# Half of the gate and up weight chunks turned by VectorE out of a blocked copy in DRAM, in an AdaLN FFN kernel

## The reference, cut to what matters

```python
def _L0_cond_ref(x, c, weight, c_weight, bias):     # x [128, 32, 512]
    out = lax.conv_general_dilated(x, weight, window_strides=(1,), padding=[(4, 4)],
                                   dimension_numbers=('NCH', 'OIH', 'NCH'), feature_group_count=4)
    ctx = jnp.einsum('nd,od->no', c, c_weight)
    return out + ctx[:, :, None] + bias[None, :, None]

def _L0_ffn_ref(x, W_gate, W_up, W_down):           # W_gate, W_up [1376, 512]; W_down [512, 1376]
    xt = x.reshape(-1, x.shape[-1])
    up = xt @ W_up.T
    gate = jax.nn.silu(xt @ W_gate.T)
    return (gate * up @ W_down.T).reshape(x.shape[:-1] + (W_down.shape[0],))

return x + _L0_ffn_ref(_L0_cond_ref(x, cond_128, ...), W_gate, W_up, W_down)
```

## Time and profile before

| | |
|---|---|
| time, median of 3 runs | 752.04 us (751.13 to 752.36) |
| the profiled execution | 751.72 us, of which its span is 749.9 us |
| PE busy | 739.6 us (99%) |
| DVE, ACT, POOL busy | 379.5, 274.4, 52.4 us |
| granted TensorE clock, mean | 0.999 |
| DMA | 152.37 MB, 203 GB/s over the span |

### The profile page before, as it was taken

How to read it: one execution, slowest core, us unless ns; L and a number is a source line. 1 busy time by engine, 2 the same in 40 slices (tenths; PEclk the granted TensorE clock), 3 DMA queues, 4 the chain that set the end, 5 groups by cost and what they waited for, 6 DMA issues and landing times.

```text
span 749.9 us, 10087 instructions
## 1 busy us (share of the span) xinstructions
PE 739.6 (99%) x3375; PEld 602.4 (80%) x3375; DVE 379.5 (51%) x639; ACT 274.4 (37%) x521; POOL 52.4 (7%) x88
## 2 busy tenths in 40 slices
PE   7999999999999999999999999999999999999998
PEld 6778888878888888887888888887888888887886
DVE  3896766654765454436734545443753333334224
ACT  4565655543433233234322333324431332333221
POOL 4433323210000000000000000000000000000000
PEclk9999999999999999999999999999999999999999
DMA  6496578569977677765544866866443967775413
GB/s 186 114 317 239 187 273 281 186 226 327 354 268 247 216 222 219 197 205 159 167 135 171 282 202 193 244 194 180 162 133 106 312 190 196 194 193 172 141 29 112
DMA packets 115029, 152.37 MB, mean 203 GB/s; under 512 B 12482, under 2 KB 50530, under 8 KB 114978
## 3 DMA queue, kind: packets, MB, share of 16 engines
q1 hardware_dynamic: 114496, 151.51, 64.8%
q10 hardware_dynamic: 482, 0.21, 0.1%
HBM read 108.95 MB, written 34.34 MB: 191 GB/s over the span
## 4 chain that ended last, share of the span: by engine, by line
PE 94%; DVE 2%; DMA 1%; SPq 1%; issue 1%; ACT 1%; POOL 0%; POOLq 0%; DVEq 0%
PE bank L727 55%; PE bank L790 32%; PE bank L645 3%; PE bank L640 3%; SPq L344 1%; PE bank L683 1%; DVE hc_lo L1091 1%; DMA x_in<-in_x 1%; PE bank L606 1%; PE bank L654 1%; PE bank L665 0%; DMA stage<-g_all 0%; DVE g_all L1294 0%; DVE ring L1091 0%; DVE g_all L1192 0%
## 5 line engine op out<-in xcount | busy, mean ns | idle before, releaser
L727 PE MATMUL bank<-hc_hi,ring 128*128 128x512 f32 (+1 forms) x1204 | 374.0, 392 | 1.0 <-issue 1.0
L727 PEld LDWEIGHTS bank<-hc_hi,ring 128*128 128x128 f32 (+1 forms) x1204 | 221.4, 185 | 50.2 <-issue 1.4
L727 PE MATMUL bank<-hc_lo,ring 128*128 128x512 f32 (+1 forms) x602 | 234.8, 390 | 0.0
L790 PE MATMUL bank<-ring,g_hi 128*128 128x512 f32 (+1 forms) x704 | 218.6, 392 | 0.0
L790 PEld LDWEIGHTS bank<-ring,g_hi 128*128 128x128 f32 (+1 forms) x704 | 131.2, 188 | 28.1 <-DVE g_lo L1091 0.8
L859 ACT ACTIVATE mix<-bank 128x512 f32<-128x512 f32 (+1 forms) x129 | 76.7, 594 | 188.0 <-PE bank L727 188.0
L790 PE MATMUL bank<-ring,g_lo 128*128 128x512 f32 (+1 forms) x352 | 137.1, 390 | 0.0
L727 PEld LDWEIGHTS bank<-hc_lo,ring 128*128 128x128 f32 (+1 forms) x602 | 111.5, 185 | 25.8
L1091 DVE TENSOR_TENSOR g_lo<-g_all,g_hi 128x512 fp32r<-128x512 f32 (+1 forms) x88 | 60.4, 689 | 88.6 <-ACT g_hi L859 88.6
L859 ACT ACTIVATE g_hi<-g_all 128x512 fp32r<-128x512 f32 (+1 forms) x88 | 55.1, 629 | 114.1 <-PE bank L790 114.0
L1265 DVE TENSOR_TENSOR mix<-bank,mix 128x512 f32<-128x512 f32 (+1 forms) x43 | 29.7, 691 | 129.4 <-PE bank L727 129.4
(11 more groups left out here) (141 smaller groups left out, 468.7 us busy)
## 6 DMA issues: line engine op xcount, KB each, us to landing
ring<-saved SPq DMA_DIRECT2D x319, 256.0 KB, 3.0
saved<-ring SPq DMA_DIRECT2D x99, 256.0 KB, 3.7
g_all<-in_x SPq DMA_DIRECT2D x32, 256.0 KB, 3.6
out_y<-g_all SPq DMA_DIRECT2D x32, 256.0 KB, 3.7
x_in<-in_x SPq DMA_DIRECT2D x96, 64.0 KB, 2.1
stage<-win SPq DMA_DIRECT2D x96, 64.0 KB, 2.9
w_nat<-in_L_ffn_W_gate SPq DMA_DIRECT2D x10, 256.0 KB, 3.4
w_nat<-in_L_ffn_W_up SPq DMA_DIRECT2D x10, 256.0 KB, 3.4
```

The lines of the kernel that those rows point to most:

```text
L727: mm = pe.matmul(bank[0:w, :], wt, hv, start=fresh and q == 0 and t == 0, stop=q == 1 and t == 2, skip_group_check=not fresh)
L790: mm = pe.matmul(acc(half, tt)[:], gs, wd, start=f == 0 and t == 0, stop=f == FC - 1 and t == 2)
```

## The change

Three things change.

1. Chunks 0 to 4 are turned by PE as before, chunks 5 to 10 (`LATE` = 5) by DVE. For them ACT issues twelve DRAM-to-DRAM DMAs in the steps `k` = 0 to 3 of the prologue (`quarter`), which write W_gate and W_up from row 640 on into a DRAM tensor `quarters`, where the elements of L stand in four blocks, one for each 32 partitions. Eight of them have 1472 rows of 256 bytes (two of these eight 240 bytes), four have 736 rows of 16 bytes. `load_nat` reads `quarters` for these chunks and waits for all six DMAs of its kind, and DVE's `turn_weights` writes `x_gate` and a new tile `up_kept`. PE's turns, ACT's copy from the bank and POOL's `wrap` go for these chunks.
2. In every group the elements of L lie otherwise on the partitions of `stage`: a half of L goes as pairs, even elements in one tile and odd ones in the other. A window's DMA writes 8 partitions with 8 KB each, where it wrote 16 with 4 KB each. PE's turns of chunks 0 to 4 read `w_nat` with a step of two elements.
3. There are two semaphores for `stage` in place of four: one for each half of L. What waited for one tile now waits for both tiles of its half.

The core of the diff:

```diff
+        quarters = nc.dram_tensor("quarters", [2, 4, F, 2 * 2 * QUAD], F32, kind="Internal").ap()
+            up_kept = sb("up_kept", [P, KC, P], F32, early)
+        staged = [half for half in (sem("staged_low"), sem("staged_high")) for _ in range(2)]
-        STAGED = JJ * LD
+        STAGED = 2 * JJ * LD
         def stage_window(queue, grp, i, w):
-            queue.dma_start(stage[w * R:(w + 1) * R, i, :, :].rearrange("r o n -> r (o n)"), windows(grp, i)[:, w, :]
-                            ).then_inc(staged[i], LD)
+            h, row = (i * JJ + w) // (2 * JJ), (i * JJ + w) % (2 * JJ) * R // 2
+            queue.dma_start(stage[row:row + R // 2, 2 * h:2 * h + 2, :, :].rearrange("r i o n -> r (i o n)"), windows(grp, i)[:, w, :]
+                            ).then_inc(staged[2 * h], LD)
...
+                    if f >= LATE:
+                        sp.wait_ge(quartered[kind], 6 * LD)
+                        size = w // QUAD * P
+                        sp.dma_start(w_nat[:, slot, 0:size], quarters[kind, :, f * P:f * P + w, :].rearrange("a (n b) e -> a n (b e)", n=QUAD)
+                                     ).then_inc(nat_loaded[slot], LD)
...
-                    if g == 0 and f + 2 < FC:
+                    if g == 0 and f + 2 < LATE:
                         turn_gate(f + 2)
...
+            def quarter(kind, a):
+                rows, part = (w_gate, w_up)[kind][LATE * P:F, :], quarters[kind, a, LATE * P:F, :]
+                at, size = PAD + 2 * QUAD * a, 2 * QUAD - (PAD if a == 3 else 0)
+                act.dma_start(part.rearrange("f (h e) -> (f h) e", h=2)[:, 0:size],
+                              rows.rearrange("f (h l) -> (f h) l", h=2)[:, at:at + size]).then_inc(quartered[kind], LD)
+                if a == 3:
+                    for h in range(2):
+                        act.dma_start(part[:, (h + 1) * 2 * QUAD - PAD:(h + 1) * 2 * QUAD], rows[:, (1 - h) * (L // 2):(1 - h) * (L // 2) + PAD]
+                                      ).then_inc(quartered[kind], LD)
             for k in range(STEPS):
                 if k + 2 < STEPS:
                     split_x(0, k + 2)
+                if k < 4:
+                    for part in range(2):
+                        quarter(k // 2, k % 2 * 2 + part)
...
+            def turn_weights(f, kind):
+                w, slot = width(f), (2 * f + kind) % NNAT
+                dve.wait_ge(nat_loaded[slot], LD * ((2 * f + kind) // NNAT + 1))
+                if kind == 0:
+                    dve.wait_ge(t_done[T1], f)
+                    dve.wait_ge(t_done[T4], f)
+                else:
+                    dve.wait_ge(t_done[T2], f)
+                dve.transpose((x_gate, up_kept)[kind][:, :, 0:w].rearrange("p i (n b) -> p b i n", n=QUAD),
+                              w_nat[:, slot, 0:w // QUAD * P].rearrange("p (c j i) -> p c i j", j=QUAD, i=2)).then_inc((gate_turned, up_turned)[kind], 1)
...
                     up_b(n, f)
                     if last and g == 0:
                         split_down(1)
+                    if g == 0 and LATE <= f + 2 < FC:
+                        turn_weights(f + 2, 0)
+                        turn_weights(f + 2, 1)
                     up_a(n, f)
```

More of the change, by code:

```diff
@@ L36, in adaln_ffn @@
     LD = 16
+    LATE = 5
+    QUAD = 32
     assert N == P and CG == 8 and R == 16 and KC == 4 and QN % 2 == 0 and G * CG == conv_w.shape[0]
@@ L139, in adaln_ffn, with up_of @@
         copy0, copy2, copy4, act_a, act_b = (mix[:, n, :] for n in range(5))
+        def up_of(f):
+            return up_kept if f >= LATE else up_ps[:].rearrange("p (i f) -> p i f", i=KC)
         def down_nat(f):
@@ L343, in stage_window, with wait_staged, nat_places @@
         def stage_window(queue, grp, i, w):
-            queue.dma_start(stage[w * R:(w + 1) * R, i, :, :].rearrange("r o n -> r (o n)"), windows(grp, i)[:, w, :]
-                            ).then_inc(staged[i], LD)
+            h, row = (i * JJ + w) // (2 * JJ), (i * JJ + w) % (2 * JJ) * R // 2
+            queue.dma_start(stage[row:row + R // 2, 2 * h:2 * h + 2, :, :].rearrange("r i o n -> r (i o n)"), windows(grp, i)[:, w, :]
+                            ).then_inc(staged[2 * h], LD)
+        def wait_staged(engine, grp, k):
+            engine.wait_ge(staged[k // 4 * 2], LD * (2 * JJ * grp + WB * (k % 4 + 1)))
+        def nat_places(f, kind, i):
+            at = PAD + i // 2 * (L // 2) + i % 2
+            return w_nat[0:width(f), (2 * f + kind) % NNAT, at:at + 2 * P - 1:2]
         block = ctx.enter_context(nc.Block())
@@ L366, in load_nat @@
                         sp.wait_ge((gate_turned, up_turned)[kind], f - NNAT // 2 + 1)
-                    sp.dma_start(w_nat[0:w, (2 * f + kind) % NNAT, 0:L], (w_gate, w_up)[kind][f * P:f * P + w, :]
-                                 ).then_inc(nat_loaded[(2 * f + kind) % NNAT], LD)
+                    slot, rows = (2 * f + kind) % NNAT, (w_gate, w_up)[kind][f * P:f * P + w, :]
+                    if f >= LATE:
[4 more added lines that the diff above has]
+                    else:
+                        sp.dma_start(w_nat[0:w, slot, 0:L], rows).then_inc(nat_loaded[slot], LD)
             def load_down(f):
@@ L653, in turn_gate @@
                 for i in range(KC):
-                    mm = pe.transpose(gate_ps[:, i * P:i * P + w], w_nat[0:w, 2 * f % NNAT, PAD + i * P:PAD + (i + 1) * P], ident[0:w, 0:w])
+                    mm = pe.transpose(gate_ps[:, i * P:i * P + w], nat_places(f, 0, i), ident[0:w, 0:w])
                 mm.then_inc(gate_turned, 1)
@@ L664, in turn_up @@
                 for i in range(KC):
-                    mm = pe.transpose(up_ps[:, i * P:i * P + w], w_nat[0:w, (2 * f + 1) % NNAT, PAD + i * P:PAD + (i + 1) * P], ident[0:w, 0:w])
+                    mm = pe.transpose(up_ps[:, i * P:i * P + w], nat_places(f, 1, i), ident[0:w, 0:w])
                 mm.then_inc(up_turned, 1)
```

23 lines of the change are left out of this document (12 added, 11 removed).

## The result

The changed kernel takes 777.63 us (776.8 to 781.13, 6 runs) beside 752.02 us of the kernel before on the same chip: 1.0354 times as long, interval 1.0329 to 1.038. That is +25.6 us; forecast were +3.7. The profiled execution took 781.09 us with a span of 779.3 us, 3.5 us above the median.

What follows compares the result with a forecast made beforehand. PE, busy in 99% of the span, was taken to bound the kernel. Terms -5.2 + 1.2 + 7.7 = +3.7 us on 751.72 gave 755.4, as a median 755.7 us; range 749.6 to 766.

Steps and rivals of the forecast that it cites:

- ACT held at its issues: Prologue: outstanding rows keep ACT at its copy DMAs, so x's seventh block is split at 30.3 us, not 22.59: +7.7 us.
- the forecast mechanism: Prologue: ACT held, the copies' price between the bytes' and the rows' bound; 751.6 to 764 us, chance 0.59.
- As many DMAs, as many bytes and rows of 512 bytes, and the issue stays what bounds them: 0: Stage DMAs in their new arrangement: still bounded by SP's issues, cost 0.
- from 60 us on the same period as before: Rounds after the prologue: expected sign in the profile, period unchanged less 0.88 us for each of six chunks.
- The removed turns: PE, chunks 5 to 10: twelve turns of four transposes at 0.44 us go, the last chunk narrower: -5.2 us.
- DVE's turns: DVE, six rounds: two transposes each, 0.7 us to twice that apiece, fit in 3.54 us of idle time: cost 0.
- The two semaphores: Prologue, second half of stage: all four splits start behind the last landing, sums one pair later: +1.2 us, lower bound 0.
- The issues alone: ACT in the prologue: twelve DMA issues, not held up, make the seventh block's split 1.9 us late; 3.4 at 0.63 each.
- short rows are dear: Rival for the copies' rows in DRAM: each costs as much as two of 512 bytes, 784 us; milder form 773; chance 0.10.

## Why the prediction was wrong

The direction, slower, was right, and ACT held at its issues was real. The size was not: +25.6 us in place of +3.7, outside the range and the forecast mechanism's own range.

- **The step that failed** is "As many DMAs, as many bytes and rows of 512 bytes, and the issue stays what bounds them: 0". Count, bytes and rows were right; but the step priced a DMA by them and left out where it writes. The issue doesn't stay what bounds them: with 8 neighbouring partitions the DMAs move at 63 GB/s where SP issues 100, a packet takes 74 ns in place of 28, SP's 30 issues take 25.9 us in place of 19.7, the last landing comes late, and 19.6 us are lost where the forecast had 1.2 with the semaphores. That it is the place is shown by the run with the partitions apart.
- **A second step that failed** is "from 60 us on the same period as before". The forecast priced the copies in the prologue alone and gave the loads out of them nothing. In the changed kernel SP is held in the rounds, PE waits there, and the rounds take 9.7 us more than without copies, which is more than the removed turns give.
- **The removed turns**, forecast -5.2, measured -5.4 alone.
- **DVE's turns**, forecast 0 at 0.7 to 1.4 us each, measured 1.08 us, and 0 on the end.
- **The two semaphores**, forecast +1.2, measured +1.1.
- **The issues alone**, forecast +1.9, measured nothing: most of them went while ACT waited anyway, and the seventh block was only 0.9 us late.
- **ACT held at its issues**, forecast +7.7 with +3.6 to +15.8 as bounds, measured +9.2 alone. The mechanism was right. The seventh block's split was put at 30.3 and came at 32.9 alone and at 32.45 in the change. But inside the change little of it reaches the end, 2.1 us at the first mark, since the prologue then waits for the stage DMAs.
- **The sum** of the parts measured alone, -5.4 + 19.6 + 9.2 = +23.4, comes near +25.6, and the 2.2 us between are no more than the runs' intervals together (that of the change alone is +24.7 to +28.6). That it comes so near is luck: about 7.5 of the 9.6 us that the copies cost ahead of the first mark are hidden in the change, and 9.7 us in the rounds, which no part has alone, stand in their place. The rounds of the changed kernel show in DVE's waits too; in the run with the new arrangement alone they are 20.3 us and hold PE up by 0.4:

```profile
DVE win L1245 <- DMA stage<-win: 28.2, 9, 6.2
```

The rival "short rows are dear" (773 to 784 us) would have come near the time with the wrong cause: the copies cost 9 to 12 us, and their rows were not slow: ACT's 9588 packets from 20 to 36 us, of 16 to 256 bytes, took 16 ns each (60.5% of 16 engines).

## What to carry to other kernels

Price a DMA by its rows, its issue and its two ends: over how many engines it goes (outermost dimension) and into which partitions. Two arrangements with the same number of DMAs, rows and bytes differed here by 17.6 us for the kernel, and a load with an outermost dimension of 4 ate 3 to 4 us of gain by what was queued behind it.

A long transfer must be put where its issuer isn't on the path, and where its rows don't meet a landing that an engine waits for. The gain appeared only when both held.

A step that is costed at nothing deserves an experiment of its own sooner than the term that looks largest.

Costs measured one by one can add up to the right total and still lie elsewhere in the whole. Marks on the busiest engine, one ahead of a stage and one behind it, show this in two lines of each trace.

## What was not expected of the hardware

- A DMA of 512-byte rows to 8 neighbouring partitions: 74 ns a packet, 65 GB/s with the engines 62% busy; to 8 partitions four apart 28 ns, and to 16 neighbouring ones with 4 KB each 29 ns.
- A transfer with outermost dimension 4 moved at 94 to 105 GB/s, and a 64 KB DMA behind it on the same queue took 10.24 us in place of 2.6 to land.
- Issues of ACT and SP are held by rows that are outstanding: on ACT two short DMAs took 2.90 us behind copies of 1472 rows, and 1.26 us behind copies of 32.
- POOL pays for the issue itself: 3.65 us for four copies of 1472 rows, 2.6 us for four loads of 512 rows, and no sign of being held by rows that are outstanding: the second four copies took 3.47 us.
- DVE's transpose of 128 x 512 with strides on both sides took 1.08 us, of x with others 0.70.
